# A gated pooling layer with a register loop on TensorE: where the loop's branch stands, and which banks set-up's bias matmuls wait for

## The reference

```python
outer = einsum('bi,bnj->bnij', cand, goods).reshape(B, N, K * K)
h1 = concatenate((broadcast(cand), goods, outer), axis=-1)     # K + K + K*K = 1088 wide
act = sigmoid(h1 @ W1 + b1)                                     # H = 36 hidden units
weight = act @ W2 + b2                                          # one number per (b, n)
out = sum(goods * weight, axis=1)                               # [2048, 32]
```

## Time and profile before

| | |
|---|---|
| median of the three runs | 270.11 us (269.48 to 270.95) |
| the profiled execution, its own time | 268.84 us |
| its span (first to last instruction) | 267.0 us |
| PE busy (matmul) | 254.5 us, 95% |
| ACT busy | 236.6 us, 89% |
| POOL busy | 196.6 us, 74% |
| DVE busy | 193.8 us, 73% |
| mean granted clock of TensorE | 0.990 |
| HBM traffic | 204 GB/s over the span |

### The profile page before, as it was taken

One profiled execution on the slowest core, in us unless ns is written; L12 is line 12 of the kernel. 1 busy time (PEld: TensorE's weight loads), 2 busy tenths in 40 slices (PEclk: granted clock), 3 DMA queues, 4 the chain that ended last, 5 costly groups with the idle time before them and its releaser, 6 DMA issues.

```text
span 267.0 us, 18217 instructions
## 1 busy us (share of the span) xinstructions
PE 254.5 (95%) x7492; PEld 150.3 (56%) x7492; DVE 193.8 (73%) x1108; ACT 236.6 (89%) x658; POOL 196.6 (74%) x349
## 2 busy tenths in 40 slices
PE   7998999999999999999999999999999999999971
PEld 2425666565565665656656666556565565665630
DVE  0890277777777877877777778777787777877886
ACT  2897999999999999999999999999999999999840
POOL 1300787887887888788788788878878878887872
PEclk9999999999999999999999999999999999999996
DMA  5880766787777777777777777777777877777200
GB/s 204 253 300 16 230 196 199 242 229 210 241 224 211 237 220 227 230 218 230 211 223 237 211 236 226 212 239 217 219 224 221 234 219 225 225 210 231 65 0 11
DMA packets 38195, 54.84 MB, mean 205 GB/s; under 512 B 4240, under 2 KB 37904, under 8 KB 38032
## 3 DMA queue, kind: packets, MB, share of 16 engines
q1 hardware_dynamic: 37872, 54.15, 67.1%
q10 hardware_dynamic: 288, 0.32, 0.3%
HBM read 54.19 MB, written 0.26 MB: 204 GB/s over the span
## 4 chain that ended last, share of the span: by engine, by line
PE 91%; ACT 2%; DMA 2%; DVE 2%; issue 1%; POOL 1%; POOLq 0%; DVEq 0%
PE z_ps L337 28%; PE w_ps L384 26%; PE x_ps L360 16%; PE s_ps L422 6%; PE x_ps L422 6%; PE z_ps L289 2%; ACT act L495 2%; DMA act<-w_outer 2%; PE s_ps L337 2%; DVE goods L535 2%; PE s_ps L289 1%; PE x_ps L289 1%; PE x_ps L302 1%; PE w_ps L289 0%; POOL top L255 0%
## 5 line engine op out<-in xcount | busy, mean ns | idle before, releaser
L495 ACT ACTIVATE act<-z_ps,bias 128x200 f32<-128x200 f32 x448 | 149.8, 441 | 13.0 <-PE z_ps L337 7.6
L535 DVE CUSTOM_DVE_ANT_0 goods<-s_ps,goods 128x200 f32<-128x200 f32 x248 | 80.5, 362 | 30.9 <-PE w_ps L422 30.9
L337 PE MATMUL z_ps<-goods,wm_ring 32*32 32x200 f32 x3360 | 77.8, 339 | 1.7 <-issue 1.6
L255 POOL TENSOR_SCALAR top<-whole,consts 128x200 bf16<-128x200 f32 x64 | 50.1, 782 | 22.4 <-DVE whole L527 16.3
L337 PEld LDWEIGHTS z_ps<-goods,wm_ring 32*32 32x32 f32 x3360 | 46.1, 103 | 20.6 <-issue 11.9
L535 DVE CUSTOM_DVE_ANT_0 goods<-x_ps,goods 128x200 f32<-128x200 f32 x124 | 40.5, 364 | 22.7 <-PE s_ps L422 22.7
L384 PE MATMUL w_ps<-act,consts 128*32 128x200 f32 x1008 | 55.7, 339 | 0.0
L360 PE MATMUL x_ps<-goods,wx 128*32 128x200 f32 x1024 | 55.3, 333 | 0.0
L259 POOL TENSOR_SCALAR mid<-rest,consts 128x200 bf16<-128x200 f32 x64 | 50.1, 782 | 6.3
L535 DVE DVE_READ_ACCUMULATOR2_ANT out_stage<- 128x1 f32 x512 | 42.6, 83 | 0.0
L482 ACT ACTIVATE wm_ring<-wm 128x256 f32<-128x256 f32 x60 | 42.4, 706 | 0.0
(11 more groups left out here) (53 smaller groups left out, 212.7 us busy)
## 6 DMA issues: line engine op xcount, KB each, us to landing
goods<-goods_t SPq DMA_DIRECT2D x256, 200.0 KB, 2.7
act<-cand_r SPq DMA_DIRECT2D x1, 1024.0 KB, 5.4
act<-cand_u SPq DMA_DIRECT2D x1, 256.0 KB, 2.8
out_t<-out_stage SPq DMA_DIRECT2D x4, 64.0 KB, 2.6
consts<-small ACTq DMA_DIRECT2D x1, 164.5 KB, 5.4
act<-w_outer ACTq DMA_DIRECT2D x1, 144.0 KB, 5.6
pick_sb<-pick SPq DMA_DIRECT2D x1, 128.0 KB, 2.8
```

The costliest lines, as they stand in the source:

```text
L255: nc.gpsimd.tensor_scalar(top[:, :], whole[:, q % 2, :], m1, None, ALU.mult).then_inc(part_step, 1)
L337: last = nc.tensor.matmul(z_bank(slot, r)[32 * c:32 * c + 32, N * s:N * s + N], weights(slot, 32 * r, 4 * s + c), goods[32 * r:32 * r + 32 ...
L495: last = nc.scalar.activation(act[:, p % A_SLOTS, r, N * s:N * s + N], z_bank(p, r)[:, N * s:N * s + N], ACT.Sigmoid, bias=bias[:, r, p, s ...
L535: last = nc.vector.tensor_tensor_reduce(goods[:, q % G_SLOTS, v, :], s_bank(q, f, s)[:, N * i:N * i + N], goods[:, q % G_SLOTS, v, :], 1.0 ...
```

## The change

PE's first loop turn begins half a pair earlier. The written-out part stops after `row_sums` of pair 3; the loop's body begins with `products_x` and `spread(.., 1)` of one pair and goes on with `products`, `spread(.., 0)` and `row_sums` of the next; the last pair's `products_x` and `spread(.., 1)` are written out behind the loop. The sequence of matmuls that PE runs is the same as before; what moves is where the jump into the loop, the ten compares with their nine jumps back and the exit stand in it. No other engine's program is changed.

The second part: the bias matmuls of set-up wait for step 7's copies out of `x_ps` and `w_ps` (x = 0 and 1), the banks that they write, in place of x = 2 and 3.

```diff
             for i in range(T_MAIN + 1):
                 step(i)
 
-            pe.wait_ge(wb_kept[0], kept(T_MAIN - 1, 2))
-            pe.wait_ge(wb_kept[1], kept(T_MAIN - 1, 3))
+            pe.wait_ge(wb_kept[0], kept(T_MAIN - 1, 0))
+            pe.wait_ge(wb_kept[1], kept(T_MAIN - 1, 1))
             pe.wait_ge(consts_loaded, 16)
...
                 if p >= 1:
                     row_sums(p, p)
-                products_x(p, p)
-                if p >= LAG:
-                    spread(p, p, 1)
+                if p < FILL - 1:
+                    products_x(p, p)
+
 
             pair, loaded = pe.alloc_register("pair"), pe.alloc_register("loaded")
-            pe.reg_mov(pair, FILL)
+            pe.reg_mov(pair, FILL - 1)
             pe.reg_mov(loaded, 64)
             with pe.Fori(0, TURNS):
-                for slot in range(FILL, FILL + RING):
-                    p = pe.snap(pair, min_val=FILL, max_val=PAIRS - 1)
-                    products(p, slot, pe.snap(loaded, min_val=64, max_val=64 * (TURNS + 1)))
-                    spread(p, slot, 0)
-                    row_sums(p, slot)
+                for slot in range(FILL - 1, FILL - 1 + RING):
+                    p = pe.snap(pair, min_val=FILL - 1, max_val=PAIRS - 1)
                     products_x(p, slot)
                     spread(p, slot, 1)
                     pe.reg_add(pair, pair, 1)
                     if slot == RING - 1:
                         pe.reg_add(loaded, loaded, 64)
+                    p = pe.snap(pair, min_val=FILL, max_val=PAIRS - 1)
+                    products(p, slot + 1, pe.snap(loaded, min_val=64, max_val=64 * (TURNS + 1)))
+                    spread(p, slot + 1, 0)
+                    row_sums(p, slot + 1)
+            products_x(PAIRS - 1, PAIRS - 1)
+            spread(PAIRS - 1, PAIRS - 1, 1)
 
             spread(PAIRS, PAIRS, 0)
             spread(PAIRS, PAIRS, 1)
```

## The result

The changed kernel takes **266.2 us** (median of six runs, 265.5 to 266.7) against 269.85 us of the kernel before in the same series (268.8 to 271.6): ratio 0.985, 95% interval 0.983 to 0.988. The profiled execution took 265.84 us, its span went from 267.0 to 264.0 us.

A forecast was written before the change was run, and what follows sets the result against it. PE's stream was taken as the bound, standing still at the loop's jumps. Jumps 3.32 + 0.37 - 10 x 0.03 = 3.39, plus 0.57 for set-up, gave 3.96 us off 270.11: 266.2 us, range 265.4 to 268.6.

The forecast's parts named there:

- What bounds the kernel; the cost of the nine jumps: PE's stream bounds the kernel; its nine jumps back before products cost 3.32 us, 0.37 each.
- The entry's 0.37 us: At the entry into PE's loop, the jump was said to cost 0.37 us over a plain pair.
- a little of it may be the first pass: In the nine jumps' 3.32 us excess, a little was allowed for the first pass through the code.
- Ten times 0.03 us left over: At ten seams moved behind row_sums, 0.03 us each was expected to stay exposed.
- 0.59: With four row-sum matmuls ahead of the jump, next row sum 0.59 us after the first: 0.18 + 0.41.
- 22.5: PE's sequencer pace, 22.5 ns for each matmul with its load, read from 68 matmuls in 1.53 us.
- 0.95: At the new place, the sequencer was to be through the jump 0.95 us after the first row sum.
- Rival 1, half hidden: Array's queue too short at the new seams: 0.10 to 0.25 us left at each, 266.9 to 268.4 us; chance 0.11.
- The bias matmuls' wait: In set-up, waiting for the earlier copies starts the bias matmuls 0.57 us sooner.
- The bound of 0.1: Low end for set-up's gain, 0.1 us: step 8's matmuls might keep the array busy.
- Rival 3, instructions loaded anew at each jump: Each jump back in PE's loop waits for an instruction load; 277 us with one packet exposed each turn; chance 0.05.
- The price of 1.2 us a packet: Cost of an instruction packet in rival 3: 11 packets took 0.3% of 16 engines' 267 us.

The follow-up runs named there:

- e4: The change with products_x of every pair in the loop put into a one-turn loop of its own; 267.70 us.
- e5: The change with products of every pair in the loop put into a one-turn loop of its own; 266.27 us.
- e2: The change with set-up's old wait, so only the loop is turned; 266.95 us, ratio 0.989 to the kernel before.
- e7: The change with the jump behind only the first n of the row sums' twelve matmuls; n = 8: 266.44 us, n = 4: 265.50, n = 1: 270.09.
- e6: The change with PE's loop head laid at a given slot of a 256-instruction block; slot 76: 268.17 us, ratio 0.993; slot 206: 267.68 us, 0.989.
- e9: The kernel before, unchanged, profiled a second time; 272.07 us.

## Why the prediction was right

Forecast 266.2 us, measured 266.2. That the two agree to a tenth is luck: the forecast gain was 3.96 us and the measured one 3.65, and the median that it was taken from, 270.11, came out as 269.85 with more runs. The mechanism was right; in the sum one term was wrong and others were off.

- *What bounds the kernel; the cost of the nine jumps* (3.32 us in the prediction): right. In three profiles of the old loop the rest, between pairs 9 and 63, was 3.2 us over, and it is 0.1 to 0.2 us over in the turned one. In the kernel before a pair with a jump takes 3.976 us and a plain one 3.629, 0.35 a jump. Measured gain 3.05 us.
- *The entry's 0.37 us*: wrong. The step "the jump into the loop has its own" took the long pair at the entry for a jump. Neither kernel's trace has a row of a jump there, e4's and e5's have none of the 60 branches ahead of their one-turn loops, and the pair is as long in the change (35.88 - 31.96 = 3.92 us, 4.37 in the second profile). It is part of the first turn's loss, which the prediction dismissed as "a little of it may be the first pass".
- *Ten times 0.03 us left over*: slightly too much, 0.01 us is left at each of nine. The mechanism (work in hand of the array against the time of the jump) was right; its sizes were not. With four matmuls ahead the load came after 0.34 us and not 0.59. In the row sums the sequencer takes 9 ns a record and not 22.5: that figure also counted the 0.28 us between the spread and `products`, whose own 64 loads start over 0.82 us, 13 ns apart. Whether the sequencer or the array sets that pace is not shown: in e5 the sequencer comes to the add behind `products` when 60 of its 64 loads have started. At the new place the sequencer is through with the jump 0.47 us after the first row sum, and not 0.95, so the cover is some 0.4 us too long, and not just enough.
- *Rival 1, half hidden*: it fell. When the jump began, 20 of the 24 matmuls of the row sums were still to start.
- *The bias matmuls' wait*, 0.57 us: the mechanism right, the size 0.70 in the profile of the change (0.64 against e2, which has the old wait: 18.26 - 16.79 = 1.47). The bound of 0.1 did not come.
- *Rival 3, instructions loaded anew at each jump*: the mechanism fell (the packets of q8 are still 11, and only one comes behind the first turn), but a first pass that costs whole microseconds was seen in both kernels; that late instructions are its cause is likely and not shown. The price of 1.2 us a packet was no bound for it: one stall took 2.6 us.

With the terms as measured: 3.05 + 0.70 = 3.75 us, against 3.65 between the medians of the timed runs. The first turn adds or takes away up to 3 us in a single execution.

## What to carry to other kernels

Put the jump of a register loop where its engine has just been given work that outlasts it, and not behind an instruction that had to wait: on PE here about 0.35 us of issued matmuls left 0.01 us of its cost (e7, n = 4), and 0.09 us left 0.33 of 0.35 (n = 1). To find such a cost, compare the cadence of one stage over many turns with that of neighbours without a jump; the list of waits showed 1.6 of the 3.2 us. The jump's own row gives the part to be covered, here some 0.2 us. And before a pass of first-time code is given a cause, take a second profile of the same kernel: here two of them differed by more than the change brought.

## What the runs showed of the hardware that was not expected

- The first pass of PE through the loop's body, 1,366 rows in the kernel before and 1,372 in the change, took 0.4 us (e6, slot 206) to 4.85 us (e6, slot 76) more than six plain pairs. Two executions of the same code differed by up to 3.3 us in it (the kernel before and e9: 22.24 and 25.56 us for pairs 3 to 9).
- The unconditional branches at the heads of 60 one-turn loops left no row in the traces of e4 and e5 (180 more instructions and not 240), and the one at the entry of the main loop none in those of the kernel before and the change. The jump over the padding in e6, slot 76, did leave one (18,278 instructions against 18,277).
- A compare on PE that is not taken has a row of 78 ns (e5, median of 60) and cost at most 0.004 us a pair there. A taken one has 0.20 to 0.25 us; it cost 0.35 us with no work in hand (the kernel before), and 0.01 with four fp32 matmuls ahead (e7, n = 4), from the second turn on.
- A jump ahead in code of first use took 2.87 us (e6, slot 76) and left the array idle for 2.6.
